# Two products of the message stage with the same gathered scalars, made by one VectorE instruction

## The reference

```
hs = xs @ w_in2f_s / sqrt(B)                 # 32 scalar features of each node
hv = einsum('nbc,bf->nfc', xv, w_in2f_v) / sqrt(B)   # 3 x 32 vector features
s, v = hs[idx_j], hv[idx_j]                  # gathered for each edge
ys, yv = Yr_ij[:, 0], Yr_ij[:, 1:4]          # the edge's own 1 + 3 numbers
Wf = ((ssp(f_ij @ W1 + b1) @ W2 + b2) * rcut).reshape(-1, F, 6)   # filters, F = 32
t_s1 = s * ys          * Wf[..., 0]          # "S"
t_s2 = (v . yv) * IS3  * Wf[..., 1]          # "VY"
t_v1 = s * yv          * Wf[..., 2]          # "AB"
t_v2 = v * ys          * Wf[..., 3]          # "V"
agg  = segment_sum([t_s1, t_s2, t_v1, t_v2], idx_i)
```

## Time and profile before

| | |
|---|---|
| Runs | 1961.87, 1964.1, 1965.44 us |
| Profiled execution | 1961.11 us, its span 1959.3 us |
| Busy over the whole span | PE 95%, DVE 66%, POOL 55%, ACT 30% |
| 1510 to 1670 us (tiles 0 to 8) | of 160 us: PE 143.5, DVE 137.2, ACT 118.9, POOL 125.0 |
| 1670 to 1930 us (tiles 9 to 24) | of 260 us: PE 246.9, DVE 254.5, ACT 215.5, POOL 202.7 |

### The profile page before, as it was taken

The page is one execution under the profiler, slowest core; times in us unless marked ns, Lnnn a source line. Parts: engine busy times, 40 slices in busy tenths (PEclk is TensorE's granted clock), DMA queues, the critical chain, the costliest instruction groups (busy, mean ns, idle before and its releaser), DMA issues. The chain is left out here.

```text
span 1959.3 us, 23685 instructions
## 1 busy us (share of the span) xinstructions
PE 1863.8 (95%) x8451; PEld 1191.1 (61%) x8451; DVE 1285.2 (66%) x1989; ACT 591.9 (30%) x1380; POOL 1075.7 (55%) x1018
## 2 busy tenths in 40 slices
PE   6799989999999999999999999999998988999996
PEld 3344445555555555555555555666665877888885
DVE  5899999869973334333333434555553988999997
ACT  1355542300000000000000000111113876888884
POOL 4000000000038878888887886188887777777773
PEclk9899999999999999999999999999998998999998
DMA  5145454322223323332332234455554344444441
GB/s 151 60 167 173 154 205 169 126 90 88 84 86 107 112 82 112 113 95 92 95 99 80 90 95 142 141 187 192 192 192 152 96 103 108 108 108 111 112 116 50
DMA packets 127305, 236.72 MB, mean 121 GB/s; under 512 B 28134, under 2 KB 70835, under 8 KB 127184
## 3 DMA queue, kind: packets, MB, share of 16 engines
q1 hardware_dynamic: 93152, 179.50, 28.6%
q0 software_dynamic: 34032, 55.66, 10.6%
HBM read 159.94 MB, written 75.11 MB: 120 GB/s over the span
## 5 line engine op out<-in xcount | busy, mean ns | idle before, releaser
L1115 PE MATMUL low<-table,abuf 125*125 125x512 f16 x3750 | 843.1, 380 | 4.8 <-DVE abuf L1554 4.8
L1115 PEld LDWEIGHTS low<-table,abuf 125*125 125x125 bf16 x3750 | 505.0, 137 | 300.0 <-issue 27.5
L957 PE MATMUL mid<-wbuf,h_t 128*125 128x512 f32 x1200 | 558.9, 602 | 6.1 <-DVE st_out L1601 4.5
L820 POOL DMA_INDIRECT by_src<-scat_row,sort x416 | 482.4, 1160 | 126.0 <-issue 118.5
L825 POOL DMA_INDIRECT table<-msg_table,wbuf x294 | 318.5, 1083 | 90.7 <-issue 81.3
L957 PEld LDWEIGHTS mid<-wbuf,h_t 128*125 128x125 f32 x1200 | 214.8, 190 | 210.3 <-issue 199.6
L812 POOL TENSOR_TENSOR scat_row<-scat_row 128x64 f32<-128x64 f32 x26 | 16.0, 615 | 524.3 <-DVE sort L1721 523.8
L1608 DVE SCALAR_TENSOR_TENSOR y<-low,inv_deg,st_in 125x512 f32<-125x512 f32 x75 | 56.2, 750 | 315.5 <-PE low L1115 198.4
L1554 DVE TENSOR_TENSOR abuf<-abuf,row_scale 125x3125 bf16<-125x3125 bf16 (+3 forms) x84 | 256.5, 3059 | 2.1 <-DMA abuf<-adj 2.0
L1149 PE MATMUL low<-table,wbuf 128*125 128x256 f32 x900 | 217.2, 392 | 31.2 <-DVE table L1851 30.7
L850 POOL DMA_INDIRECT sort<-msg_table,sort x156 | 193.0, 1237 | 82.3 <-issue 82.0
(11 more groups left out here) (215 smaller groups left out, 1636.3 us busy)
## 6 DMA issues: line engine op xcount, KB each, us to landing
abuf<-adj SPq DMA_DIRECT2D x75, 781.2 KB, 4.9
adj<-table SPq DMA_DIRECT2D x25, 781.2 KB, 4.6
states<-st_out SPq DMA_DIRECT2D x75, 256.0 KB, 2.0
st_in<-states SPq DMA_DIRECT2D x75, 256.0 KB, 4.9
early_rows<-sort POOLq DMA_DIRECT2D x30, 320.0 KB, 2.8
table<-early_rows SPq DMA_DIRECT2D x25, 384.0 KB, 6.5
by_src<-scat_row,sort POOLq DMA_INDIRECT x416
by_src<-blank SPq DMA_DIRECT2D x25, 252.0 KB, 4.0
```

The lines of the kernel that those rows point to most:

```text
L820: pool.indirect_dma_start(out=by_src, out_offset=bass.IndirectOffsetOnAxis(ap=place_i[:, k * PIECE + j:k * PIECE + j + 1], axis=0), in_=sc ...
L957: last = pe.matmul(to[0:TN, :], h_t[i % 2][:, k, :], weights[l % 2][:, a, k, :], start=k == 0, stop=k == KC - 1)
L1115: last = pe.matmul(p_agg[k % 2][0:TN, :], a_tile[k % 3][:, a, :], table[ps % 2][0:TN, a, h, :], start=a == 0 and h == 0, stop=a == TILES - ...
```

## The change

The columns of the filters stand in another order: AB, S, VY, V in place of S, VY, AB, V. AB and S are now neighbours, so one instruction can multiply the gathered scalars s (read twice through a stride of zero) with both, 64 columns for each slot. Its result and the product with V lie together in `av`, which grows by 32 columns and takes the place of `ab`. The group has six instructions, in another order: `vy` first, then the double product, then the product with V, after which `s_av` is raised. The count of `s_gd` that frees the gathered slots is now the third of a group (the sum over `vy`) and no longer the second. To put the filter columns in their new order, W2 and b2 are loaded in three pieces each, for each of the three copies: 18 DMAs in place of 6, and three entries of the list per step.

```diff
-    ab = treg.take(P, [GS, F])
+    av = [treg.take(P, [GS, F + G]) for _ in range(2)]
...
-        blocks.append((w2_sb[F * j:F * j + F, j, :], w2))
-        blocks.append((w2_sb[BLK * F:BLK * F + 1, j, :], b2.rearrange("(a f) -> a f", a=1)))
+        for lo, hi, at in FILTERS_AT:
+            blocks.append((w2_sb[F * j:F * j + F, j, at:at + hi - lo], w2[:, lo:hi]))
+            blocks.append((w2_sb[BLK * F:BLK * F + 1, j, at:at + hi - lo], b2[lo:hi].rearrange("(a f) -> a f", a=1)))
...
-                    for to, of in later[(w - 8) * 2:(w - 7) * 2]:
+                    for to, of in later[(w - 8) * 3:(w - 7) * 3]:
...
-                        pool.wait_ge(s_gd, 3 * (NG * (t - 2) + g) + 2)
+                        pool.wait_ge(s_gd, 3 * (NG * (t - 2) + g) + 3)
...
-                dve.tensor_tensor(av[n % 2][:, :, 0:F], s, w[:, :, 0, :], ALU.mult)
-                dve.tensor_tensor(av[n % 2][:, :, F:G].rearrange("p j (c f) -> p j c f", c=C3), v,
-                                  w[:, :, 3, :].unsqueeze(2).broadcast_to([P, GS, C3, F]), ALU.mult).then_inc(s_av, 1)
                 dve.tensor_tensor(vy[:, :, :, :], v, angle, ALU.mult).then_inc(s_gd, 1)
+                if n >= 2:
+                    dve.wait_ge(s_m, n - 1)
+                dve.tensor_tensor(products[:, :, 0:2 * F].rearrange("p j (k f) -> p j k f", k=2), s.unsqueeze(2).broadcast_to([P, GS, 2, F]),
+                                  w[:, :, W_AB:W_S + 1, :], ALU.mult).then_inc(s_gd, 1)
+                dve.tensor_tensor(products[:, :, 2 * F:F + G].rearrange("p j (c f) -> p j c f", c=C3), v,
+                                  w[:, :, W_V, :].unsqueeze(2).broadcast_to([P, GS, C3, F]), ALU.mult).then_inc(s_av, 1)
                 dve.wait_ge(s_m, n)
-                dve.tensor_tensor(ab[:, :, :], s, w[:, :, 2, :], ALU.mult).then_inc(s_gd, 1)
                 dve.wait_ge(s_gd, 3 * n + 1)
                 dve.tensor_reduce(vys[:, :, :], vy[:, :, :, :].rearrange("p j c f -> p j f c"), AX.X, ALU.add).then_inc(s_gd, 1)
```

More of the change, by code:

```diff
@@ L29 @@
 KC = D // P
+W_AB, W_S, W_VY, W_V = range(4)
 B, F, R, YD, C3 = 128, 32, 20, 4, 3
@@ L37 @@
 G = 4 * F
+FILTERS_AT = (2 * F, 3 * F, 0), (0, 2 * F, F), (3 * F, 4 * F, 3 * F)
 LOG2 = 0.6931471805599453
@@ L267, in gnn_kernel @@
     msg_slots = [treg.take(P, [SLOTS, G]) for _ in range(2)]
-    av = [treg.take(P, [GS, G]) for _ in range(2)]
-    ab = treg.take(P, [GS, F])
+    av = [treg.take(P, [GS, F + G]) for _ in range(2)]
     vy = treg.take(P, [GS, C3 * F]).rearrange("p j (c f) -> p j c f", c=C3)
@@ L433, in gnn_kernel @@
     s_xs = sem("extra_sums_stored")
-    X_PE, X_ACT, X_DVE = 2 + 2 * NG, 4 + NG, 4 + 7 * NG
+    X_PE, X_ACT, X_DVE = 2 + 2 * NG, 4 + NG, 4 + 6 * NG
     RS_B = 1.0 / float(B) ** 0.5
@@ L737, in load_early @@
                 if t >= 2:
-                    sp.wait_ge(s_gd, 3 * NG * (t - 2) + 2)
+                    sp.wait_ge(s_gd, 3 * NG * (t - 2) + 3)
                 c, i = t // FEW, t % FEW
@@ L1343, in scaled @@
                 for j in range(GS):
-                    last = act.activation(msg[n % 2][:, j, 0:G], av[n % 2][:, j, :], ACT.Copy, scale=win_p[t % 3][:, g * GS + j, PAY_Y:PAY_Y + 1])
+                    last = act.activation(msg[n % 2][:, j, 0:G], av[n % 2][:, j, F:F + G], ACT.Copy, scale=win_p[t % 3][:, g * GS + j, PAY_Y:PAY_Y + 1])
                 last.then_inc(s_av2, 1)
@@ L1378, in extra_round @@
                 for g in range(NG):
-                    wait_alone(act, s_xd, d0 + 5 + 7 * g)
+                    wait_alone(act, s_xd, d0 + 5 + 6 * g)
                     for j in range(GS):
-                        last = act.activation(msg[0][:, j, 0:G], av[0][:, j, :], ACT.Copy, scale=x_win[:, g * GS + j, PAY_Y:PAY_Y + 1])
+                        last = act.activation(msg[0][:, j, 0:G], av[0][:, j, F:F + G], ACT.Copy, scale=x_win[:, g * GS + j, PAY_Y:PAY_Y + 1])
                     last.then_inc(s_xa, 1)
@@ L1837, in group @@
                 to = msg[n % 2]
-                dve.tensor_tensor(av[n % 2][:, :, 0:F], s, w[:, :, 0, :], ALU.mult)
-                dve.tensor_tensor(av[n % 2][:, :, F:G].rearrange("p j (c f) -> p j c f", c=C3), v,
-                                  w[:, :, 3, :].unsqueeze(2).broadcast_to([P, GS, C3, F]), ALU.mult).then_inc(s_av, 1)
+                products = av[n % 2]
                 dve.tensor_tensor(vy[:, :, :, :], v, angle, ALU.mult).then_inc(s_gd, 1)
+                if n >= 2:
[4 more added lines that the diff above has]
+                                  w[:, :, W_V, :].unsqueeze(2).broadcast_to([P, GS, C3, F]), ALU.mult).then_inc(s_av, 1)
                 dve.wait_ge(s_m, n)
-                dve.tensor_tensor(ab[:, :, :], s, w[:, :, 2, :], ALU.mult).then_inc(s_gd, 1)
                 dve.wait_ge(s_gd, 3 * n + 1)
@@ L1848, in group @@
                     dve.wait_ge(s_hot, n - 1)
-                dve.scalar_tensor_tensor(out=to[:, :, G:G + F], in0=vys[:, :, :], scalar=IS3, in1=w[:, :, 1, :],
+                dve.scalar_tensor_tensor(out=to[:, :, G:G + F], in0=vys[:, :, :], scalar=IS3, in1=w[:, :, W_VY, :],
                                          op0=ALU.mult, op1=ALU.mult).then_inc(s_w_free, 1)
                 dve.tensor_tensor(to[:, :, G + F:2 * G].rearrange("p j (c f) -> p j c f", c=C3),
-                                  ab[:, :, :].unsqueeze(2).broadcast_to([P, GS, C3, F]), angle, ALU.mult).then_inc(s_m, 1)
+                                  products[:, :, 0:F].unsqueeze(2).broadcast_to([P, GS, C3, F]), angle, ALU.mult).then_inc(s_m, 1)
             def sum_pairs(t):
@@ L1916, in extra_round @@
                         wait_alone(dve, s_xp, p0 + 2 + 2 * g)
-                    cd.link(dve.scalar_tensor_tensor(out=msg[0][:, :, G:G + F], in0=vys[:, :, :], scalar=IS3, in1=w[:, :, 1, :], op0=ALU.mult, op1=ALU.mult))
+                    cd.link(dve.scalar_tensor_tensor(out=msg[0][:, :, G:G + F], in0=vys[:, :, :], scalar=IS3, in1=w[:, :, W_VY, :], op0=ALU.mult, op1=ALU.mult))
                     cd.link(dve.tensor_tensor(msg[0][:, :, G + F:2 * G].rearrange("p j (c f) -> p j c f", c=C3),
-                                              ab[:, :, :].unsqueeze(2).broadcast_to([P, GS, C3, F]), angle, ALU.mult))
+                                              av[0][:, :, 0:F].unsqueeze(2).broadcast_to([P, GS, C3, F]), angle, ALU.mult))
                 wait_alone(dve, s_xp, p0 + X_PE)
```

12 lines of the change are left out of this document (6 added, 6 removed).

## The result

The changed kernel takes 1956.68 us (median of 13 runs, 1954.07 to 1961.01), the kernel before 1962.32 us (13 runs, 1958.37 to 1966.62). The ratio is 0.9972, 95% interval [0.9962, 0.9982]. That is 5.6 us faster. The profiled execution took 1957.87 us (span 1956.0).

The account below looks back on a forecast made before the run. A DVE-PE loop of 16.57 us a tile bounds the steady stretch, POOL tiles 3 to 8. Steady -0.3, last groups -0.3, tiles 0 to 8 -1.2: -1.8 from 1964.1 gives 1962.3 us; 8-in-10 range 1957.5 to 1967.

Parts of the forecast that it names:

- Tiles 3 to 8: Tiles where POOL sets the time: fewer gathers held by DVE, -1.2 us, ends -9.9 and +5.2.
- I count it as hit in one tile of three: Group 2, tiles 3 to 8: the gather at S + 0.97 falls inside the old `vy`; 6 x 0.2 us.
- The number of such products in a tile does not change: Products with two SBUF inputs that hold gathers stay ten a tile; only where they stand changes.
- Rival 2: POOL gets clear of DVE in tiles 3 to 8, two thirds of 9.9 us go: 1956.9 us, chance 0.18.
- The 9.9 us of lost time: POOL's 84 steps in tiles 3 to 8 took 114.9 us against 105.0 unheld; 9.9 lost to DVE.
- The base: Median of the kernel before taken as 1964.1 us, 3.0 above the profiled execution; the forecast starts there.
- The double product: One DVE instruction for two in each group: 0.47 us start to start, group shorter by about 0.07 us.
- ACT as the later one: Group 2, steady tiles: ACT ends 0.11 us behind DVE, PE's start +0.05; -0.02 a tile, -0.3 over 15 tiles.
- Waits, loads in the setup: New and moved waits, and twelve further DMAs inside SP's wait: no cost; without that cover the loads cost 6 us.
- 1 (every group counts): DVE is the bound after all, 75 groups at 0.07 us make 5.2 us: 1958.9 us, chance 0.12.
- 3: POOL becomes the bound in the steady stretch, losing over 1.57 us a tile: 9 us slower, 1973, chance 0.08.
- 4: ACT is later than worked out: every 0.1 us beyond 0.11 costs 1.5 us; chance 0.05.

Follow-up runs that it names:

- the second pair: Second profiled executions of the kernel before and the changed kernel, both unchanged, on two different chips: 1961.91 and 1955.71 us.
- g4: The kernel before run once more unchanged, for a second profiled execution: 1961.91 us in one run.
- f7: The changed kernel with five gathers instead of six in groups 1 and 2 from tile 2 on: 1947.03 us, ratio 0.9927.
- f6: The kernel before with five gathers instead of six in groups 1 and 2 from tile 2 on: 1944.51 us, ratio 0.9915.
- h2: The changed kernel with its last product early and its one-hot product reading node numbers from PSUM: 1955.76 us, ratio 0.9971.
- e2: The kernel before with the double product alone, `vy` left third: 1959.86 us, ratio 0.9983.
- f5: The changed kernel with another group order, last product early and two products with two SBUF inputs back to back: 1974.03 us, ratio 1.0066.
- f8: The kernel before with the second input of `vy` taken from PSUM: 1951.96 us, ratio 0.995.
- e8: The kernel before with the second input of `vy` from PSUM, on the chip where the kernel before takes 2101.07 us: 2123.21 us, ratio 1.0112.

## Why the prediction was wrong

**Tiles 3 to 8: the term that failed.** I took -1.2 us from ends of -9.9 and +5.2, and POOL's time fell by 5.8 (6.5 in the second pair). The mechanism was right: a gather at about S + 1 is held by the old `vy` and not by the new one. The price was a little high: the earlier trace rows cost 0.59, and the mean of all such holds is 0.4. The count was wrong. "I count it as hit in one tile of three", two hits, had group 2 of one tile read closely. The table has 11 and 14 such holds in six tiles before: 3 and 5 in group 2, 3 and 3 in group 1, and 5 and 6 in group 0, where DVE waits for nothing and where I had looked for none.

In group 0 it was not a matter of chance, as I had priced it. POOL and then DVE, right behind the held gather of tile 3 shown above:

```profile
1577.44 0.94 POOL L825 DMA_INDIRECT table<-msg_table,wbuf  x1 [0.30 <-issue]
1578.69 0.95 POOL L825 DMA_INDIRECT table<-msg_table,wbuf  x1 [0.30 <-issue]
1579.94 1.28 POOL L825 DMA_INDIRECT table<-msg_table,wbuf  x1 [0.30 <-issue]
```

```profile
1578.73 0.35 DVE L1838 TENSOR_TENSOR table<-table,mid 128x192 f32<-128x192 f32 x1
1579.00 0.75 DVE L1839 TENSOR_TENSOR table<-table,mid 128x576 f32<-128x576 f32 x1
1579.66 0.75 DVE L1841 TENSOR_TENSOR table<-table,wbuf 128x576 f32<-128x576 f32 x1
```

A gather held by `vy` ends at S + 2.51, whenever it began. The third gather from there begins 2.80 us later, at S + 5.31. Group 0 opens at S + 4.10, so that gather falls on its S + 1.21 and is held again. Three of the five holds in group 0, and five of the six in g4, stand behind a held gather of group 2.

I also left the one-hot at its old price, "The number of such products in a tile does not change". With line 1727 it fell from 13 holds (4.9 us) to 2 (1.1 us), about as much as `vy` gave, and the last product took over some, at a lower price (10 for 6). Rival 2 had the mechanism and named 1956.9; it had a chance of 0.18. The 9.9 us of lost time in the prediction were 11.4, since two of the 84 steps are stores, together about 1.4 us shorter than two gathers.

**The base.** The forecast and the measured time are 5.6 us apart. 1.8 of them are the base, 1964.1 from three runs where thirteen gave 1962.32; the other 3.8 are the gain.

**The double product: right.** 0.47 us start to start, 0.07 a group.

**ACT as the later one: right in kind, short in size.** I allowed 0.05 us from ACT's end to PE's start, as from DVE; it is 0.14. The steady tile became 0.05 longer and not 0.02 shorter: +0.8 over 15 tiles in place of -0.3.

**Waits, loads in the setup: no cost that can be told.** The loads went into SP's wait, as I had it; the row beside the earlier trace rows is now

```profile
SPq L546 <- DVE st_out L1603: 137.8, 18, 9.3
```

Group 1 of tile 3 comes 1.3 and 0.7 us later (1.0 in f7 against f6). But it scatters by as much: 1564.66 and 1565.75 in two executions of the kernel before, and from 1563.4 (h2) to 1568.7 (e2) in kernels with the added loads, so a part may be theirs or nothing.

**The end: not foreseen.** PE's last sums or the products behind them run at a lower clock there, +1.8 and +1.0 us in the two pairs. Whether that comes from the change is open, as said above.

**Rivals.** 1 (every group counts) is refuted by f6 and f7. 3 did not occur here (POOL loses 1.64 us a tile, just what a tile of 16.62 leaves, and DVE waits for no gather in nearly all tiles), though f5 shows that such a loss costs what it said: 1973 was named, 1974.03 measured. 4 occurred in small.

Open: why the two parts together lose less than each alone, beyond the table; why the one-hot product holds fewer gathers; and whether the change has a part in the later tile 3 and the longer end.

## What to carry to other kernels

An instruction that gathers on one engine can be held by what another engine reads, so for a stage at the gatherer's pace ask of every product which memories it reads and where it starts against the gathers, not only how long it is. Where a held instruction ends at a fixed distance behind its holder, hits can repeat at the same offset: count them over all tiles of the stage in the trace before pricing them, since one tile read closely is no rate. And run the version in which the suspected engine is never late: it parts the saving of work from the saving of phase, which a plain timing adds up.

## What the runs showed of the hardware

- A gather's 0.945 us becomes up to 1.68 in the kernel before when it begins while a VectorE product with both inputs in SBUF runs, and it ends 0.8 us behind that product. With one input of `vy` in PSUM, `vy` holds no gather: mean 1083 to 992 ns.
- A held gather leaves POOL in step with DVE: the third gather behind one held in group 2 begins 1.21 us into group 0 and is held again, 3 and 5 times in six tiles.
- Reading the one-hot's node numbers from PSUM in place of SBUF costs VectorE nothing: 929 and 930 ns for 750 elements.
- PE starts 0.14 us behind ACT's last scaling, and 0.04 behind DVE's last product: 1758.77 to 1758.81.
- Two chips differed by 7% on the same kernel before (2101 and 1961 us), and the ranking of the variants changed with it: the kernel with `vy` reading PSUM won 0.5% on one (f8) and lost 1.1% on the other (e8).
- The twelve sums behind the same idle time of PE (1.68 us) took 2.83 us at 2.4 GHz in one execution of the kernel after and 4.51 us in the other, where the granted clock fell to 1.2 GHz.
